# Finding rows by one-hot matmuls: 5 tiles by 20 high values in place of 4 by 25, and type matrices in two parts in place of three

## The reference, cut to what matters

```python
# layer 0, two attention layers (3 heads of 32, then 1 head of 32)
h = (x @ W).reshape(N, heads, outc)
alpha_s = (h * a_s).sum(-1); alpha_d = (h * a_d).sum(-1)
e = leaky_relu(alpha_s[src] + alpha_d[dst], 0.2)
m = segment_max(e, dst, N); p = exp(e - m[dst]); z = segment_sum(p, dst, N)
out = segment_sum(h[src] * (p / z[dst])[:, :, None], dst, N) + b
# layer 1, two relation layers: x_src @ W[edge_type] / count, summed over dst
x_src = x[src]
# layer 2, a sheaf layer (not touched by the change)
# layer 3, typed attention: one 16x16 matrix for each of 90 edge types
h_src = h[src]
e = concatenate([h_src @ Ws.T, he @ Ws.T, h[dst] @ Ws.T]) @ Wa.T
msg = einsum('ei,eio->eo', h_src, W_rel[rel_type]) * e
h_out = segment_sum(msg, dst, N)
```

## Time and profile before

| | us |
|---|---|
| Median of 3 runs | 25884.65 (25847.85 to 25956.43) |
| Profiled execution, its own time | 25623.17 |
| Its span | 25621.4 |
| PE busy | 20516.3 (80%) |
| DVE busy | 19514.0 (76%) |
| POOL busy | 14540.6 (57%) |
| ACT busy | 12983.4 (51%) |
| Mean granted clock | 0.914 |

### The profile page before, as it was taken

The page is one execution under the profiler, slowest core; times in us unless marked ns, Lnnn a source line. Parts: engine busy times, 40 slices in busy tenths (PEclk is TensorE's granted clock), DMA queues, the critical chain, the costliest instruction groups (busy, mean ns, idle before and its releaser), DMA issues. The chain is left out here.

```text
span 25621.4 us, 355895 instructions
## 1 busy us (share of the span) xinstructions
PE 20516.3 (80%) x110397; PEld 18475.2 (72%) x110397; DVE 19514.0 (76%) x36629; ACT 12983.4 (51%) x15054; POOL 14540.6 (57%) x14357
## 2 busy tenths in 40 slices
PE   0688875888884899969999458888888889499996
PEld 0577764888883788858888348888888888278885
DVE  4699995778774899969999436666666667599997
ACT  0455541333331566636666236666666667266664
POOL 1555545556553555545555556666666764455555
PEclk9999996999996999979999768999999999599998
DMA  5222221111111111111111111111111111522221
GB/s 91 57 74 74 70 69 25 39 40 44 41 38 29 39 40 40 40 35 35 36 36 36 17 16 19 19 18 19 19 19 19 19 19 13 149 72 72 68 71 50
DMA packets 1347468, 1106.65 MB, mean 43 GB/s; under 512 B 937658, under 2 KB 1197972, under 8 KB 1320180
## 3 DMA queue, kind: packets, MB, share of 16 engines
q1 hardware_dynamic: 673364, 571.63, 8.1%
q0 software_dynamic: 545440, 167.01, 7.8%
q10 hardware_dynamic: 127872, 358.35, 3.8%
HBM read 646.52 MB, written 448.94 MB: 43 GB/s over the span
## 5 line engine op out<-in xcount | busy, mean ns | idle before, releaser
L987 PE MATMUL gat_e_found<-gat_e_parts,gat_e_lowhot 128*128 128x400 f32 x27776 | 5629.2, 358 | 997.9 <-DVE gat_e_rows L951 511.4
L987 PEld LDWEIGHTS gat_e_found<-gat_e_parts,gat_e_lowhot 128*128 128x128 f32 x27776 | 5147.1, 194 | 1479.5 <-DVE gat_e_rows L951 718.9
L1105 POOL DMA_INDIRECT gat_e_rows<-att_t,gat_e_index x3968 | 3765.6, 949 | 2761.2 <-issue 1421.0
L1980 PEld LDWEIGHTS rgcn_e_found<-rgcn_e_parts,rgcn_e_lowhot 128*128 128x128 f32 x23808 | 4298.3, 188 | 674.7 <-DVE rgcn_e_picked L1825 444.2
L760 POOL DMA_INDIRECT rgcn_e_rows<-rel_t,rgcn_e_index x3472 | 3279.6, 945 | 2520.6 <-DMA rgcn_e_rows<-rel_t,rgcn_e_index 1149.9
L1980 PE MATMUL rgcn_e_found<-rgcn_e_parts,rgcn_e_lowhot 128*128 128x400 f32 x23808 | 4547.0, 348 | 180.3 <-DVE rgcn_e_picked L1825 131.1
L2541 PE MATMUL sheaf_e_bysrc<-sheaf_e_exacthot,sheaf_e_masked 128*128 128x392 f32 x19840 | 4246.4, 372 | 413.7 <-ACT sheaf_e_exacthot L2644 349.9
L2272 POOL DMA_INDIRECT sheaf_e_rows<-sheaf_t,sheaf_e_index x3224 | 3386.7, 1050 | 1724.7 <-issue 886.0
L2541 PEld LDWEIGHTS sheaf_e_bysrc<-sheaf_e_exacthot,sheaf_e_masked 128*128 128x128 f32 x19840 | 3867.4, 207 | 523.5 <-ACT sheaf_e_exacthot L2644 383.9
L2644 ACT CAST sheaf_e_exacthot<-sheaf_e_eighthhot 128x1568 fp32r<-128x1568 bf16 x2480 | 3587.2, 1500 | 924.4 <-DVE sheaf_e_eighthhot L2355 541.7
L987 PE MATMUL typed_e_found<-typed_e_parts,typed_e_lowhot 128*128 128x400 f32 x11904 | 2371.7, 352 | 334.0 <-DVE typed_e_hrows L951 242.6
(11 more groups left out here) (515 smaller groups left out, 27987.5 us busy)
## 6 DMA issues: line engine op xcount, KB each, us to landing
rgcn_e_low<-few_low_d SPq DMA_DIRECT2D x124, 768.0 KB
typed_e_types<-in_type_t SPq DMA_DIRECT2D x62, 1536.0 KB
sumsatt<-gat_e_sums ACTq DMA_DIRECT2D x62, 1404.0 KB
typed_t<-typed_p_y SPq DMA_DIRECT2D x98, 765.0 KB
sumsatt<-gat_e_sums ACTq DMA_DIRECT2D x62, 1092.0 KB
gat_e_rows<-att_t,gat_e_index POOLq DMA_INDIRECT x3968
rgcn_e_rows<-rel_t,rgcn_e_index POOLq DMA_INDIRECT x3472
sumsrel<-rgcn_e_sums ACTq DMA_DIRECT2D x124, 416.0 KB
```

Of the source, the lines that this page charges most:

```text
L987: last = pe.matmul(self.found_of(a, n)[:, c + b, 0:w], hot[:, k, col * P:(col + 1) * P], self.table.column(part, k)[:, b * w:(b + 1) * w], ...
L1105: pool.indirect_dma_start(rows_t[a.k][:, j, :], None, table, rows(index[a.k][:, j:j + 1]))\
L1980: last = pe.matmul(found_ps[c // 2][:, c % 2, 0:FHI * FD], low_hot[at % 2][:, n, c * P:(c + 1) * P], short.column(part, n), start=n == 0 a ...
```

## The change

The fetches by one-hot in the attention, relation and typed passes cut a node number in another place: the low part is one of 5 tiles (below 640) and the high part one of 20 values. The moving operand of a matmul goes from 16x25 = 400 to 16x20 = 320 columns, and a column takes 5 x 2 = 10 matmuls (20 in gat2). What DVE picks from goes from 800 to 640 elements for two columns, ACT's distances from 4 to 5 for a group and its relu from 2048 to 2560 elements. Since 640 is no power of two, the stage that splits the ids gets the tile by a division by 5, written as a product with 205 and a shift by 10. In the typed pass the type matrices are held in two float32r parts, not three bf16 ones, and the one-hot of the type becomes float32r. The number of columns that are gathered and found stays as it was, as do the loops and the waits.

```diff
-FLO, FLOW, FLOG = 4, 512, 9
+FLO, FLOW = 5, 640
...
-                dve.tensor_scalar(whole[:, :], src[:, :], FLOG, None, ALU.logical_shift_right)
-                o.link(dve.tensor_scalar(masked[:, :], by_column[:, :], FLOW - 1, None, ALU.bitwise_and))
-                dve.tensor_copy(few_high[:, :], whole[:, :]).then_inc(few_ready, 1)
-                o.link(dve.tensor_copy(few_low[:, :], masked[:, :]))
-                dve.sem_inc(few_ready, 1)
...
+                def divide(t, at, part):
                     o.link(dve.tensor_scalar(t[:, :], at[:, :], 7, None, ALU.logical_shift_right))
-                    o.link(dve.tensor_scalar(t[:, :], t[:, :], SEVENTH, None, ALU.mult))
+                    o.link(dve.tensor_scalar(t[:, :], t[:, :], part, None, ALU.mult))
                     o.link(dve.tensor_scalar(t[:, :], t[:, :], 10, None, ALU.logical_shift_right))
-                dve.tensor_copy(high[:, :], src[:, :]).then_inc(high_ready, 1)
+                divide(whole, by_column, FIFTH)
+                divide(masked, src, FIFTH)
+                dve.tensor_copy(few_high[:, :], masked[:, :]).then_inc(few_ready, 1)
+                o.link(dve.scalar_tensor_tensor(few_low[:, :], whole[:, :], -float(FLOW), by_column[:, :], ALU.mult,
+                                                ALU.add))
+                dve.sem_inc(few_ready, 1)
+                divide(whole, by_column, SEVENTH)
+                divide(masked, src, SEVENTH)
...
-def quarters(g, even=False):
-    return Cut(FLO, FHI + FHI % 2 if even else FHI, g.few_low_d, g.few_high_d, 2, F32R)
+def fifths(g):
+    return Cut(FLO, FHI, g.few_low_d, g.few_high_d, 2, F32R)
...
-        self.type_hot = [s.sb(f"typehot{k}", [P, QC * P], BF16) for k in range(2)]
+        self.type_hot = [s.sb(f"typehot{k}", [P, QC * P], F32R) for k in range(2)]
...
-        self.kinds = s.sb("kinds", [P, 3, FD, FD], BF16)
+        self.kinds = s.sb("kinds", [P, 2, FD, FD], F32R)
...
-            for part in range(3):
+            for part in range(2):
                 last = pe.matmul(self.kind_ps[n % 2][:, c, :, :].rearrange("p o i -> p (o i)"),
```

## The result

The changed kernel takes 26237.58 us (median of 4 runs, 26202.12 to 26248.61) against 25870.78 (4 runs), ratio 1.0135, interval 1.0113 to 1.0157. The forecast was 25280, with a range that ended at 25755.

The account below looks back on a forecast made before the run. No single engine was taken to bound the program; the bound differed by pass. gat1 -50, gat2 -267, rgcn0 -37, rgcn1 -31, typed -230 and splits +14 sum to -601 us: 25884.65 becomes about 25280, range 25035 to 25755.

Parts of the forecast that it names:

- PE's stream: gat2: PE's loads and matmuls in a chunk go from 47.4 us to 320 x 0.150 = 48.0 us.
- the slow stretches: gat2: chunks where single PE matmuls wait only for their issue; mean excess 4.8 us a chunk, kept in the forecast.
- rival B: gat2: slow stretches grow with 64 more matmuls a chunk and eat its gain; -334 us in all, 25550; chance 0.25.
- The reason given against rival B: Relation passes: rgcn issues as densely at clock 1.00 without the slow stretches; no size of its own.
- rgcn0 and rgcn1, forecast -37 and -31: Relation passes, PE-bound: PE +0.5 us a chunk, shorter picking frees 1.1 of waits; -0.6 and -0.5 a chunk.
- The pair: PE: a float32 load and matmul of 320 columns takes 150 ns, against 185 ns at 400 columns.
- rival A: PE: load and stream add up, 170 ns for each load and matmul; +600 us, 26480, slower; chance 0.08.
- DVE and ACT: Per chunk: DVE saves 4.0 us in gat1, relation passes and typed, 5.3 in gat2; ACT gains 6.4 with 24 columns, hidden.
- gat1's gain: gat1: POOL stays the bound while DVE and PE get out of its way; -0.8 us a chunk, -50, between 0 and -150.
- typed, forecast -230: Typed pass: DVE 43.4, PE 42.4; POOL's floor of 45.6 plus 0.8 of joints gives 46.4 us a chunk, -3.7.
- rival C: POOL and ACT take over sooner: gat1 0, typed 48.0 us a chunk, gat2 55.4; -384 us, 25500; chance 0.20.
- the matrices: Typed pass: type matrices in two float32 parts save PE 3.5 us a chunk, alone worth nothing there, making room for +0.5.

## Why the prediction was wrong

**gat2: the step that failed.** The prediction took PE's stream as 48.0, waits 1.5, and the slow stretches as a fixed excess of 4.8 us a chunk, "I take 48.0 + 1.5 of waits + 4.8 = 54.3". The stream was right (47.0). The term of 4.8 was not: it was carried over from before as if the change could not move it. Without open gathers the pass stands 45 us above its bare stream in all; in the changed kernel it stands 1271 above it, 20.5 us a chunk where the sum has 6.3. Here are both kernels on one chip, Z, from the first to the last matmul of the finding in gat2. The pace is 183 and 147 ns for each matmul, and each row below it says how much longer its matmuls took than that:

| us | before | changed |
|---|---|---|
| All matmuls at the pace | 2904 | 2916 |
| Slow steps | 217 | 529 |
| Other matmuls that waited for issue | 236 | 342 |
| Other matmuls at half clock | 180 | 405 |
| Waits for DVE and ACT | 289 | 115 |
| All the rest | 79 | 50 |
| Sum | 3905 | 4357 |

PE does wait 174 us less for DVE and ACT, as the prediction hoped; slow steps, waits for issue and half clock give back 643. The half clock comes with the pauses over the kernels above (55 us of it with four gathers, 1792 with a drain of 12). The signs that were named ahead did show: the mean chunk of gat2 is 4221 / 62 = 68.1 us, over the 57 that spoke for rival B, and gat2 and typed together lose time where they were to give 250. The earlier trace rows was such a step and it was in the argument: rival B spoke of it, said rightly that issues are what the change adds, and then priced it at the lost gain, 267, so that -334 was left in all; it cost that gain and 445 to 558 us more in gat2 alone.

**The reason given against rival B was false.** "rgcn issues as densely at clock 1.00 without them" was nearly true at 183 ns. At 147 ns rgcn0 shows 77 us of slow steps and rgcn1 37 (some 14 and 6 before, same chip), and at 183 ns with the changed kernel's number of instructions none. I had read off the density before the change, at 183 ns, and let it stand for the density after it. That the distance alone decides is not shown: gat1 had no fewer steps at 183 ns.

**rgcn0 and rgcn1, forecast -37 and -31, were +76 and +59** on one chip. The bare stream costs PE almost the same as before (240 x 0.147 = 35.3 us a chunk, 192 x 0.183 = 35.1), less than the +0.5 forecast. In the first pair of executions, where rgcn0 grew by 46 us, the waits for picking did shrink, from 69.6 us to 27.1, but the waits for issue grew from 28.8 to 66.2 in their place, and waits for ACT's table, 18.8, are new. These three come to 14 us more and the stream to some 12; the other 20 of the 46 stay open. How large it is depends on the chip: on Y, with 20 to 24 us of slow steps, the relation passes of the changed kernel take 2849 to 2859 us and those of 4 by 25 take 2841 and 2825. PE's waits in rgcn0 of the changed kernel, first execution:

```profile
PE rgcn_e_found L1983 <- issue: 66.2, 102, 3.2
...
PE rgcn_e_found L1983 <- DVE rgcn_e_picked L1828: 27.1, 59, 1.4
PE rgcn_e_found L1983 <- ACT rgcn_e_lowhot L2048: 18.8, 26, 1.1
```

**The pair** was forecast at 150 ns and is 147, 0.80 of 183: between these two widths only the columns count. Of the Trainium skill's two rules in "TensorE: Matmul & The Clock Gate", section "Back-to-back issue gap", the formula (136 ns) is 11 ns low, and the spacing set by both operations, whose shape was rival A, does not show at these widths.

**DVE and ACT** came out as worked: gat1's gain, 85 us on Z and 9 in the first pair, lies in its range (0 to 150).

**typed, forecast -230, gave -144** (2951, 47.6 us a chunk, rival C's 48.0). DVE 43.4 as forecast, PE 42.9 for 42.4. The missing step is that three engines within 4 us of each other do not stand on POOL's floor of 45.6 + 0.8: DVE, which had waited 11.5 us for PE in typed, now waits 104 (in other executions than these), and POOL still waits 153.4 us for DVE where fewer than 60 were named as the sign. In the sum the matrices were put at nothing for time; with DVE faster they were worth 62 us. Per matmul they cost 474.4 / 2976 = 159 ns busy, the upper end of the bounds.

**The base.** The profiled execution of before was the shortest of that kernel's; with gat2 between 3607 and 3882 us by chip and execution, its slow steps were already 6 to 8% of the pass and hid in "4.8".

**Still open** is what the steps are. They are not seen as fetching of PE's program: the queues that carry instructions moved 13 packets, 0.16 MB, in 3200 us of gat2. SP also has instructions of registers and branches that last 0.7 us, but they do not follow the steps: there are 187 of them in gat2 of the changed kernel and 109 before, on Z 51 and 166, and with a drain of 12, where the steps are most, 3. The runs show that open gathers slow PE's issue, and not by what. That the shorter distance is what makes the change suffer is borne out in the relation passes and typed, contradicted in gat1, and for gat2, where the loss is, only argued. Nor is it shown that the half clock follows from the pauses alone, since no run had one without the other.

## What to carry to other kernels

Cutting matmuls finer at the same number of columns was free for TensorE's stream here only where nothing else slowed its issue; before doing so, look in the timeline for single matmuls that waited for "issue", and ask what else is open at that moment. If it is indirect DMAs, drain them more often first: that one number was worth 765 us of gat2 on one chip, more than the 601 forecast for the whole change. A stall that appears in a profile as an average excess is not a constant to carry over: ask what it depends on and whether the change moves that. And where a stall differs from chip to chip as this one does, compare on one chip only.

## What the runs showed of the hardware that was not expected

- With nine gathers issued since the last drain PE issues loads and matmuls in steps of 0.5, 0.7 and 1.4 us; with a drain after every 12 and with 4 gathers in all a chunk the waits for issue in the same stream are 1073 and 25 us on one chip, with a drain after every 9 and every 6 they are 677 and 354 on another.
- The size of it hangs on the chip: gat1 of the changed kernel shows about 160 us of slow steps on one and 30 to 50 on another.
- A float32r pair of 128x128 weights and 320 columns follows the last at 147 ns, of 400 at 183: proportional to columns.
- A float32r matmul of 256 columns is busy for 159 ns, a bf16 one for 138: two float32r parts save 0.10 us of PE a column over three bf16 parts, a quarter.
